# Row maxima of the attention scores formed once per quad of heads instead of once per half quad

## The reference, cut to what matters

```
x = x + L0_xattn(layernorm(x), ctx, mask)     # A: softmax(q k / 4, masked) v, W, b
x = x + L0_ffn(layernorm(x))                  # hadamard, 4-bit activations, ternary weights
x = x + L1_xattn(layernorm(x), ctx, bias)     # C: softmax(q k / 4 + bias) v, then FFN of 1024
x = x + L1_ffn(layernorm(x))                  # 8 experts, each with its best 512 tokens
```

## Time and profile before

| | |
|---|---|
| median of 3 runs | 980.29 us (979.94 to 981.11) |
| profiled execution, its own time | 980.22 us |
| span from first to last instruction | 978.4 us |
| layers' loop, about | 14 to 710 us |
| TensorE, VectorE, ScalarE, GpSimd busy | 86%, 68%, 40%, 47% of the span |
| granted TensorE clock, mean | 0.928 of 2.4 GHz |

### The profile page before, as it was taken

How to read it: one execution, slowest core, us unless ns; L and a number is a source line. 1 busy time by engine, 2 the same in 40 slices (tenths; PEclk the granted TensorE clock), 3 DMA queues, 4 the chain that set the end, 5 groups by cost and what they waited for, 6 DMA issues and landing times.

```text
span 978.4 us, 17867 instructions
## 1 busy us (share of the span) xinstructions
PE 838.1 (86%) x7077; PEld 607.1 (62%) x7077; DVE 668.6 (68%) x1501; ACT 387.6 (40%) x594; POOL 456.7 (47%) x403
## 2 busy tenths in 40 slices
PE   6888777989999998998998978998733499999995
PEld 4556444555666665665665655666622399999985
DVE  4654677887898898897798586683266466666441
ACT  1323222335335435434434413423110266666662
POOL 4444235445356456356245234152320467777742
PEclk9999889989999999999999988989955599999998
DMA  9320643443353443443434325240050135555531
GB/s 296 115 60 12 242 168 101 153 168 118 137 175 118 150 167 120 156 167 115 157 107 143 107 110 194 88 150 11 33 183 0 44 114 130 134 129 132 135 71 22
DMA packets 47697, 120.57 MB, mean 123 GB/s; under 512 B 4737, under 2 KB 33921, under 8 KB 39425
## 3 DMA queue, kind: packets, MB, share of 16 engines
q1 hardware_dynamic: 41472, 111.06, 33.4%
q0 software_dynamic: 6144, 8.39, 4.8%
HBM read 111.05 MB, written 8.39 MB: 122 GB/s over the span
## 4 chain that ended last, share of the span: by engine, by line
PE 57%; DVE 25%; issue 7%; ACT 4%; POOL 3%; DMA 2%; SPq 0%; POOLq 0%; DVEq 0%
PE row_scores L437 9%; PE ps_v L525 7%; PE row_scores L1289 5%; PE ps_m L543 4%; PE ps_v L1306 4%; PE ps_r L1306 4%; DVE row_max L653 4%; DVE probs L683 3%; PE ps_v L407 3%; DVE row_scores L660 3%; PE ps_m L414 2%; PE ps_r L507 2%; PE key_scores L457 2%; DVE attnT_A L692 2%; DVE attnT_C L692 2%
## 5 line engine op out<-in xcount | busy, mean ns | idle before, releaser
L972 POOL TENSOR_TENSOR probs<-probs 128x512 f32<-128x512 f32 x128 | 162.0, 1271 | 121.9 <-ACT probs L841 94.8
L841 ACT ACTIVATE probs<-probs 128x1024 f32<-128x1024 f32 x64 | 67.7, 1057 | 230.6 <-DVE probs L683 230.5
L660 DVE CUSTOM_DVE_ANT_0 row_scores<-row_scores,bias_q 128x256 f32<-128x256 f32 x256 | 100.5, 453 | 42.3 <-PE row_scores L437 42.0
L838 ACT ACTIVATE probs<-key_scores 128x1024 f32<-128x1024 f32 x64 | 65.5, 1024 | 129.8 <-PE key_scores L453 129.1
L653 DVE TENSOR_REDUCE row_max<-row_scores 128x4 f32<-128x1024 f32 x64 | 78.2, 1221 | 45.5 <-PE row_scores L437 45.4
L683 DVE TENSOR_TENSOR probs<-key_scores,bias_k 128x1024 f32<-128x1024 f32 x64 | 77.8, 1216 | 8.9 <-PE key_scores L453 8.7
L437 PE MATMUL row_scores<-k_op_c,q_op_C 32*128 32x256 f32 x512 | 76.4, 418 | 6.0 <-DVE row_max L660 6.0
L437 PE MATMUL row_scores<-k_op_a,q_op_A 32*128 32x256 f32 x512 | 73.8, 404 | 8.0 <-DVE q_op_C L669 7.4
L453 PE MATMUL key_scores<-q_op_C,k_op_c 32*128 32x256 f32 x512 | 76.5, 417 | 0.4 <-DVE q_op_C L669 0.4
L453 PE MATMUL key_scores<-q_op_A,k_op_a 32*128 32x256 f32 x512 | 74.4, 408 | 0.0
L1371 POOL TENSOR_TENSOR w_l<-w1e,w_h 128x512 fp32r<-128x512 f32 x32 | 52.2, 1661 | 42.8 <-ACT w_h L1322 42.8
(11 more groups left out here) (242 smaller groups left out, 2163.2 us busy)
## 6 DMA issues: line engine op xcount, KB each, us to landing
bias_q<-in_bias_q SPq DMA_DIRECT2D x32, 1024.0 KB, 4.9
bias_k<-in_bias_k SPq DMA_DIRECT2D x32, 1024.0 KB, 4.9
w1e<-in_w1e SPq DMA_DIRECT2D x8, 1024.0 KB, 5.1
w2e<-in_w2e SPq DMA_DIRECT2D x8, 1024.0 KB, 6.7
k_op_a<-in_k_a SPq DMA_DIRECT2D x32, 128.0 KB, 2.3
mask_int<-in_mask SPq DMA_DIRECT2D x8, 512.0 KB, 5.8
v_op_A<-in_v_a SPq DMA_DIRECT2D x8, 512.0 KB, 5.4
w<-in_w SPq DMA_DIRECT2D x2, 1024.0 KB, 10.2
```

The lines of the kernel that those rows point to most:

```text
L660: ins = nc.vector.tensor_tensor_reduce(row_scores[:, j, qt * SEQ:(qt + 1) * SEQ], row_scores[:, j, qt * SEQ:(qt + 1) * SEQ], bias_q[:, m % ...
L838: nc.scalar.activation(of, key_scores[:, :, :], ACT.Exp).then_inc(exp_done, 1)
L841: nc.scalar.activation(of, of, ACT.Exp).then_inc(exp_done, 1)
L972: nc.gpsimd.tensor_tensor(both[:, :, 0, :], both[:, :, 0, :], both[:, :, 1, :], ALU.add).then_inc(blocks_summed, 1)
```

## The change

- The pair of transposes (pe_maximum_rows) and the addition (ve_add_maximum) are made once for a quad, over all 128 partitions, at the even step 2 pos, when both halves' maxima are there. max_rows and max_added count quads.
- The scores of a quad come at steps 2 pos + 1 and 2 pos + 2 instead of 2 pos and 2 pos + 1; exponentials, bias additions and sums follow, the values come at 2 pos + 4 instead of 2 pos + 3. Maxima stay where they were. So in the main part the steps hold in turn: C maxima with C scores, C maxima with A scores, A maxima with A scores, A maxima with C scores. Where both are C, pe_scores_apart is taken.
- A half is always the heads 0 and 1 or 2 and 3 in this order (group is gone). row_max has two tiles per parity instead of three, and two memsets fewer.
- The four tables and the moved jobs have new steps.

```diff
-MAX_TILE = {(q, half): (2 * [p for p in ORDER if p.par == q.par].index(q) + half) % 3 for q in ORDER for half in range(2)}
+MAX_TILE = {q: [p for p in ORDER if p.par == q.par].index(q) % 2 for q in ORDER}
-    return 2 * values_place(kind, b, c) + 1
-PE_SLOT = {"wb": -5, "wa": 0, "T_A": -32, "wv": 18, "wo": 35, "T_B": 3, "had": 4, "T_F": 39, "T_q": 6, "tern": 8, "f1_0": 40,
-           "T_R": 58, "f1_1": 42, "lg": 59, "f1_2": 43, "wk": 12, "T_C": 13, "f1_3": 45, "wq": 14,
-           "f2_0": 46, "f2_1": 50, "f2_2": 52, "f2_3": 53, "f2_4": 53, "f2_5": 53, "f2_6": 54, "f2_7": 54}
-VE_SLOT = {"wb0": -10, "wb1": -9, "wb2": -8, "wb3": -7, "stA": -35, "mask": -32, "apA": -34, "x1": 0, "apB": 2, "y": 35,
-           "quant": 4, "qcap": 5, "apF": 37, "yf": 54, "apG": 55, "yq": 8, "stR": 56, "apR": 57, "stC": 10, "apC": 11,
-           "lgc": 59}
-AC_SLOT = {"wb": -5, "qA": -32, "vC": 18, "hbT": 3, "zT": 39, "qT": 6, "xrT": 58, "g0": 42, "kC": 12, "xcT": 13, "g1": 45,
-           "qC": 14}
-PO_SLOT = {"rsA": -35, "xb": -34, "rsB": 0, "rsF": 35, "yb": 37, "rsG": 54, "aff": 55, "x2": 8, "rsR": 56, "rsC": 10,
-           "xe": 12, "mk": -21}
+    return 2 * PLACE[Quad(kind, b, 2 * c + 1)] + 4
+PE_SLOT = {"wb": -4, "wa": 1, "T_A": -31, "wv": 19, "T_B": 4, "had": 5, "wo": 38, "T_F": 41, "T_q": 7, "tern": 8, "wk": 9,
+           "f1_0": 43, "f1_1": 44, "T_C": 13, "f1_2": 45, "wq": 14, "f1_3": 46, "T_R": 63, "lg": 64,
+           "f2_0": 47, "f2_1": 49, "f2_2": 51, "f2_3": 52, "f2_4": 52, "f2_5": 53, "f2_6": 54, "f2_7": 55}
+VE_SLOT = {"wb0": -10, "wb1": -9, "wb2": -8, "wb3": -7, "stA": -35, "mask": -32, "apA": -34, "x1": 1, "apB": 3,
+           "quant": 5, "qcap": 6, "y": 38, "yf": 55, "apF": 39, "yq": 9, "apG": 57, "stR": 59, "stC": 11, "apC": 12, "apR": 61,
+           "lgc": 65}
+AC_SLOT = {"wb": -4, "qA": -31, "vC": 19, "hbT": 4, "zT": 41, "qT": 7, "kC": 9, "g0": 44, "xcT": 13, "qC": 14, "g1": 46,
+           "xrT": 63}
+PO_SLOT = {"rsA": -35, "xb": -34, "rsB": 1, "rsF": 38, "yb": 39, "rsG": 55, "x2": 9, "aff": 57, "rsR": 59, "rsC": 11,
+           "xe": 13, "mk": -20}
...
-move(0, stA=-32, rsA=-32, apA=-31, xb=-31, T_A=-30, qA=-30, wa=2, x1=2, rsB=2, apB=2, T_q=5, qT=5, qcap=4, tern=6, yq=6,
-     x2=6, wk=7, kC=7, stC=7, rsC=7, apC=8, T_C=8, xcT=8, wq=8, qC=8, xe=9)
+move(0, stA=-32, rsA=-32, apA=-31, xb=-31, T_A=-30, qA=-30, wa=3, x1=3, rsB=3, apB=3, T_B=4, hbT=4, had=5, quant=5, qcap=5,
+     T_q=6, qT=6, tern=7, yq=7, x2=7, wk=8, kC=8, stC=8, rsC=8, apC=9, T_C=9, xcT=9, wq=9, qC=9, xe=10)
...
-        row_max = [[lay(f"row_max_{par}{n}", [P, QT, P]) for n in range(3)] for par in range(2)]
+        row_max = [[lay(f"row_max_{par}{n}", [P, QT, P]) for n in range(2)] for par in range(2)]
...
-        def group(quad, half):
-            return (PLACE[quad] - 1 + half) % 2
-        def previous_half(step):
-            pos, half = divmod(step - 1, 2)
-            return quad_of(pos + 1), half
+        def maximised_at(step):
+            return quad_of(step // 2 + 1), step % 2
+        def scored_at(step):
+            return quad_of((step - 1) // 2), (step - 1) % 2
+        def rows_at(step):
+            return quad_of(step // 2) if step % 2 == 0 else None
+        def valued_at(step):
+            q = quad_of(step // 2 - 2) if step % 2 == 0 else None
+            return q if q is not None and q.par == 1 else None
...
-                pe.wait_ge(max_added, half_number(now, half) + 1)
+                pe.wait_ge(max_added, number(now) + 1)
...
-        def pe_maximum_rows(pe, q, half):
-            n = half_number(q, half)
-            pe.wait_ge(max_taken, n + 1)
-            wait(pe, max_added, n)
+        def pe_maximum_rows(pe, q):
+            pe.wait_ge(max_taken, 2 * number(q) + 2)
+            wait(pe, max_added, number(q))
             for qt in range(QT):
-                ins = nc.tensor.matmul(ps_r[:, qt * P:(qt + 1) * P], row_max[q.par][MAX_TILE[q, half]][:, qt, :], ident[:, :],
+                ins = nc.tensor.matmul(ps_r[:, qt * P:(qt + 1) * P], row_max[q.par][MAX_TILE[q]][:, qt, :], ident[:, :],
                                        start=True, stop=True, is_transpose=True)
             ins.then_inc(max_rows, 1)
...
-        def ve_add_maximum(ve, q, half):
-            g = group(q, half)
-            r = slice(64 * g, 64 * g + 64)
-            ve.wait_ge(max_rows, half_number(q, half) + 1)
-            nc.vector.tensor_tensor(queries(q)[r, :], ps_r[r, 0:SEQ], queries(q)[r, :], ALU.add).then_inc(max_added, 1)
+        def ve_add_maximum(ve, q):
+            ve.wait_ge(max_rows, number(q) + 1)
+            nc.vector.tensor_tensor(queries(q), ps_r[:, 0:SEQ], queries(q), ALU.add).then_inc(max_added, 1)
...
+            g = half
...
-                pos, half = divmod(step, 2)
-                now, then, past = quad_of(pos), quad_of(pos + 1), quad_of(pos - 1)
-                maximised, of_half = previous_half(step)
+                (now, of_now), (then, of_then) = scored_at(step), maximised_at(step)
...
-                if maximised is not None:
-                    ve_add_maximum(ve, maximised, of_half)
+                if rows_at(step) is not None:
+                    ve_add_maximum(ve, rows_at(step))
...
-                if half == 1 and past is not None and past.par == 1:
-                    ve_normalise(ve, past)
+                if valued_at(step) is not None:
+                    ve_normalise(ve, valued_at(step))
```

More of the change, by code:

```diff
@@ L111 @@
[L111 to L121, removed]
+move(4, f2_0=112, f2_1=112, f2_2=113, f2_3=113, f2_4=113, f2_5=114, f2_6=114, f2_7=114, yf=115, rsG=115, apG=116, aff=116,
+     stR=118, rsR=118, apR=119, T_R=122, xrT=122, lg=123, lgc=123)
@@ new lines @@
+move(5, wo=115, y=115, rsF=115, apF=116, yb=116, T_F=118, zT=118, f1_0=119, f1_1=121, g0=121, f1_2=122, f1_3=123, g1=123,
+     f2_0=125, f2_1=125, f2_2=126, f2_3=126, f2_4=127, f2_5=127, f2_6=128, f2_7=128, yf=128, rsG=128, apG=129, aff=129,
+     stR=130, rsR=130, apR=131, T_R=132, xrT=132, lg=133, lgc=133)
+move(6, wv=117, vC=117, wo=125, y=125, rsF=125, apF=126, yb=126, T_F=129, zT=129, f1_0=130, f1_1=131, g0=131, f1_2=132,
+     f1_3=133, g1=133, f2_0=134, f2_1=134, f2_2=134, f2_3=134, f2_4=135, f2_5=135, f2_6=135, f2_7=135, yf=136, rsG=136,
+     apG=137, aff=137, stR=138, rsR=138, apR=139, T_R=140, xrT=140, lg=141, lgc=141)
@@ new lines @@
+move(7, wa=113, x1=113, rsB=113, apB=113, T_B=114, hbT=114, had=115, quant=115, qcap=115, T_q=116, qT=116, tern=117, yq=117,
+     x2=117, stC=118, rsC=118, apC=118, T_C=119, xcT=119, wq=120, qC=120, xe=119, wk=121, kC=121, wv=125, vC=125, wo=135,
+     y=135, rsF=135, apF=136, yb=136, T_F=137, zT=137, f1_0=138, f1_1=138, f1_2=138, f1_3=138, g0=138, g1=138, f2_0=139,
+     f2_1=139, f2_4=140, f2_5=140, f2_2=141, f2_3=141, f2_6=142, f2_7=142, yf=142, rsG=142, apG=143, aff=143, stR=144,
+     rsR=144, apR=145, T_R=146, xrT=146, lg=147, lgc=147)
@@ L457, in pe_mask, with pe_round @@
             nc.tensor.matmul(bank, ident_b[:, :], mask_bf[:, q.b % 2, way, :], start=True, stop=False)
-        def pe_round(pe, now, then, half):
+        def pe_round(pe, now, of_now, then, of_then):
             if then is not None:
-                pe_wait_maximum(pe, then, half)
+                pe_wait_maximum(pe, then, of_then)
                 if then.kind == A:
@@ L465, in pe_round @@
             if now is not None:
-                pe_wait_scores(pe, now, half)
+                pe_wait_scores(pe, now, of_now)
                 if now.kind == A:
@@ L481, in pe_round, with pe_scores_apart @@
                 ins_now.then_inc(scores_ready, 1)
-        def pe_scores_apart(pe, now, then, half):
-            pe_wait_maximum(pe, then, half)
+        def pe_scores_apart(pe, now, of_now, then, of_then):
+            pe_wait_maximum(pe, then, of_then)
             if then.kind == A:
@@ L488, in pe_scores_apart @@
             for t in range(QT):
-                for j in heads_of(group(then, half)):
+                for j in heads_of(of_then):
                     ins_then = pe_maximum_scores(then, j, t)
             ins_then.then_inc(max_scores, 1)
-            pe_wait_scores(pe, now, half)
+            pe_wait_scores(pe, now, of_now)
             if now.kind == A:
@@ L640, in pe_layers @@
                     pe_keep_busy(24, ps_m[1])
-                if -11 <= step <= 8 and step != -5:
+                if -11 <= step <= 8 and step != -4:
                     pe_keep_busy(8, ps_m[1])
@@ L649, in ve_take_maximum @@
             first = DK * (1 - q.par)
[L650 to L651 removed]
+            g = half
+            of = row_max[q.par][MAX_TILE[q]][:, :, :].rearrange("p t (j r) -> p j t r", j=4)[:, 2 * g:2 * g + 2, :, first]
             if q.kind == A:
@@ L915, in ac_layers @@
             for step in range(2 * FIRST, 2 * LAST):
-                pos, half = divmod(step, 2)
-                now = quad_of(pos)
+                now, of_now = scored_at(step)
                 if now is not None:
```

(6 more changed lines are left out.)

47 lines of the change are left out of this document (20 added, 27 removed).

## The result

The changed kernel takes 1020.14 us, the median of four runs (1014.32 to 1023.94); the kernel before took 980.18 us beside it. The ratio is 1.040, 95% interval 1.036 to 1.044: slower, as forecast, and inside the range.

The account below looks back on a forecast made before the run. TensorE was taken as the bound; start 2.5, steps 16 to 31 2.5, steps 32 to 47 3.6, full stretches 23.8 and end 2 summed to 34.4 us on 980.2: 1015 us, range 988 to 1032.

Parts of the forecast that it names:

- What bounds the kernel, and what the change removes: TensorE bounds full stretches; 64 transpose pairs go, 17.3 us of TensorE, and 64 additions, 27 us of VectorE.
- The table's forced waits: New table orders make TensorE wait: wk for yq 2.0 to 2.8 us, T_A for lgc 2.4, T_B for vC 0.4.
- The steps with C and C: Steps with C maxima and C scores split into half rounds, priced at 0 to 1.13 us a step.
- One sign of the prediction: In the new trace, TensorE's idle time in a full stretch up by about 8 us, its length 79 to 82.
- g0 ahead of an A exponential: Step 13 of a full stretch: ScalarE's g0 delays an exponential that the next masks need, 0.9 us.
- The end: Late bias_q load, one more half round and eight pairs fewer: together +2 us, bounds -4 and +8.
- The bias_q behind a bias_k: Batch 7's last C quad waits for a bias_q load queued behind a bias_k now a step later: +3 us.
- The start and the light stretches: Start +2.5 us from one added step less memsets; steps 16 to 31 +2.5, steps 32 to 47 +3.6.
- Rival 3: The clock falls to about 0.93 in the full stretches, 22 us more: 1026 to 1037 us; chance 0.14.
- rival 1: TensorE stays the bound and a lighter VectorE hides the waits: 965 us; chance 0.08.
- Rival 2: Only the forced waits count, all else is covered: +8, 988 us; chance 0.10.
- Rival 4: No change, waits of 7 us a stretch by chance; chance 0.04.

Follow-up runs that it names:

- e11: e8 with each pair of transposes issued twice and the addition made in two halves of 64 partitions: 993.12 us, ratio 1.0127.
- e3: The changed kernel with each pair of transposes issued twice and the addition made in two halves of 64 partitions: 1031.63 us, ratio 1.0531.
- e1: The changed kernel with wk and kC put back from step 9 to step 12 of the table: 1003.63 us, ratio 1.0225.
- e2: The changed kernel with lgc put ahead of x1 on VectorE in step 65: 1014.24 us, ratio 1.0346.
- e8: The mended kernel: e4 plus e7's order of bias loads, with wk ahead of f1_2 in step 12: 976.94 us, ratio 0.9938.
- e4: The changed kernel with the old kernel's table moved one step later, wk at 12, lgc ahead of x1: 993.21 us, ratio 1.0112.
- e5: The changed kernel with both halves in one round again in steps of C maxima and C scores: 1023.97 us, ratio 1.0415.
- e12: e8 with both halves in one round again in steps of C maxima and C scores: 981.79 us, ratio 1.0000.
- e7: The changed kernel with the last quad's bias_q loaded ahead of the previous quad's bias_k in batches 6 and 7: 1009.7 us, ratio 1.0274.

## Why the prediction was right, point by point

**What bounds the kernel, and what the change removes**: right. The saved work was worth about what the TensorE time of the transposes says, 64 x 0.27 = 17 us: putting transposes and narrow additions back costs 16 to 18 us in e11 (medians, ratios) and 11.5 us in e3, where forced waits can cover a part. No run puts only one of the two back.

**The table's forced waits**: right in place, cause and size. wk waited 2.4 us a batch (2.0 to 2.8 forecast) and T_A 1.9 (2.4). That the clock can fall behind such a wait was not counted. Removing the two orders gave 16.5 us (e1) and 5.9 us (e2). In e8 the loss is gone with rows once per quad and the lag left as they are, so it is shown that the table and the order of loads, together with the lag, made it. What e4 to e8 don't separate is which single entry beyond wk and lgc gave the rest.

**The steps with C and C**: bounds of 0 to 1.13 us for taking the halves apart; shown to be nothing or a small gain (e5, e12), because the bias of the step before ends later anyway. One sign of the prediction failed by this: TensorE's idle time in a full stretch was to rise by about 8 us and rose by 2.9. While the scores wait for the bias, the half round of the maxima keeps TensorE busy, so the waits appear as busy time. That rose by 3.0 us where 2.2 less had been taken, some 1.7 of it from the half clock behind wk (step 57 against 73); the length is as forecast. Counted as the prediction counts, length against prices, step 60 holds 6.21 - 3.61 = 2.6 us of waits, 1.3 of them idle, where 3.2 had been taken for step 12; step 61 holds 1.5 us idle where 2.0 had been taken. There g0 ahead of an A exponential was priced too high: 0.6 us, not 0.9.

**The lag**: not named as a term of its own, and no run shows a fixed price for it. e11 has the work of before with the lag and the mended table; lengths of the full stretches in us:

| stretch | before | e11 | e8 |
|---|---|---|---|
| 48 to 63 | 74.28 | 75.34 | 73.72 |
| 64 to 79 | 74.27 | 75.52 | 73.74 |
| 80 to 95 | 75.95 | 75.38 | 73.75 |
| 96 to 111 | 74.68 | 73.73 | 72.00 |
| sum | 299.18 | 299.97 | 293.21 |

Lag and table together cost 1.1 and 1.2 us in the first two, less than nothing in the last two, 0.8 us in all. Of the 6.8 us that once per quad gives in the four, 6.0 are left against the kernel before. The expected gain goes elsewhere: e8 wins 10.1 us in steps 16 to 111 and loses 1.0 at the start and 7.9 behind step 112. The light stretches tell little, as they follow the clock: e11, with more work than e8, needs 67.7 us for steps 16 to 31 at 0.91 where e8 needs 70.9 at 0.81.

**The end**: the right mechanism, mis-sized, +8.0 against +2. The bias_q behind a bias_k was put at +3. The wait itself made step 128 3.6 us longer (7.9 against 4.4), but the half clock behind the pause was not counted: the order of loads cost 7.1 us in the traces and 10 us on e7's medians. That makes it the largest single entry after wk.

**The start and the light stretches**: +0.9 and +0.3 where 2.5 and 2.5 were taken. These are terms that vary with the clock from run to run: in the traces of e2 and e7, whose tables are the changed kernel's up to step 64, step 16 begins at 109.9 and 108.0, and steps 16 to 31 last 75.9 and 76.1 us at a clock of 0.78, not 72.9 at 0.82.

```profile
109.90:185.80 75.90, 60.59 (x447) 35.21 (x452) 46.08 (x119) 20.67 (x27) 30.20 (x26) 0.78 0.39 138
577.10:695.50 118.40, 104.61 (x733) 71.41 (x732) 79.11 (x227) 36.27 (x54) 40.13 (x42) 0.84 0.35 127
```

These are e2's windows of steps 16 to 31 and of 112 to the last scores, the second 115.9 us at 0.88 in the changed kernel. Together they are 5.5 us longer, about the 6 us by which the median lies above the profiled run. It seems that the profiled run was short in both, and that the sum's agreement to 0.4 us owes something to that, too; the slower runs of the changed kernel have no trace that would show it.

**Rival 3, the clock**: in the place named, the full stretches, it did not happen: they run at 0.98 to 1.00, not 0.93. Its premise failed, too: TensorE is busy 73.5 us of 80.1, not 68. By the rule cited there (the Trainium skill, TensorE: Matmul & The Clock Gate, "A second HAM failure mode: psum-queue depth-cycling"), short pauses between groups make the clock swing; the trace agrees only behind single pauses of 1.9 us (T_A, twice), 2.4 us (wk, step 57) and 4.5 us (step 128), and not behind most of the 6 to 8 us of waits that a full stretch holds. In the stretch at 112 and in the spread of the runs the clock plays a part, some 6 us by the comparison above.

**Rivals 1, 2 and 4**: the waits were not hidden (rival 1, 965 us); even the mended kernel, with 3 to 4 us of idle time in a full stretch, gets 977. Rival 2 (988 us) had the forced waits right, but its premise that all else is covered failed: by wk's 2.4 us less 2.2 for the pairs the stretch from step 48 on would be 0.2 us longer, and it is 5.8. Rival 4, no change, falls with the result.

**Two numbers of the prediction** don't follow from its working. The lower bounds of its terms add up to 980.2 + 8 + 2 + 2 - 4 = 988 us, not 1000 (the upper ones to 1029, as said). And the 67 in rival 1's 7.3 us stands on no row: VectorE's 64.20 us less 3.4 are 60.8.
